# Two graph convolutions of a network block on one core: the sums of all destination blocks stay in seven PSUM banks, ScalarE makes the one-hots, SyncE counts landed tiles

## The chip, the cores and the metric

The program runs on one core of one Trainium2 chip. The metric is the device time of the whole program in microseconds (us), median of several runs; lower is better. The profile is one execution of the same program, recorded by the hardware profiler.

## The reference, cut to what matters

The whole reference is a two-layer network on 6250 nodes of 256 values with 100000 edges. Each layer adds a graph operator and a linear-attention mixer to the nodes, then a mixture-of-experts network. The part that changes is the graph operator of the second layer (two convolutions of width 64) and the mixer that is computed beside it:

```python
def gcn_conv(x, W, b, src, dst, n_nodes):
    h = x @ W
    deg = jax.ops.segment_sum(ones, dst, num_segments=n_nodes) + 1.0
    dinv = jax.lax.rsqrt(deg)
    norm = dinv[src] * dinv[dst]
    msg = h[src] * norm[:, None]
    agg = jax.ops.segment_sum(msg, dst, num_segments=n_nodes)
    agg = agg + h * (dinv * dinv)[:, None]
    return agg + b
h1 = jax.nn.relu(gcn_conv(embedding, W1, b1, src, dst, n))
h2 = jax.nn.relu(gcn_conv(h1, W2, b2, src, dst, n))
...
k = _ln(k, kln_g, kln_b); v = _ln(v, vln_g, vln_b)
kv = jnp.einsum('bhnd,bhne->bhde', k, v) / HW
...
h = jax.nn.gelu(ret @ w1 + b1, approximate=False)
return h @ w2 + b2 + bias
```

Everything is float32. The kernel sums rows of 64 values in both convolutions: the table of the first holds `dinv * (x @ W1)`, that of the second `dinv * relu(...)`, and `W2` is applied afterwards in another stage.

## The kernel before

The program is a row of stages with a barrier of all engines between them. `convolve` (L1806) is called twice, with `which` 0 and 1. Nodes are in `NB` = 49 blocks of 128. Edges are sorted by destination and cut into `NT` = 782 tiles of 128 edges, in `TG` = 98 groups of 8. A tile that spans two blocks is used once for each, so there are `NS` = 832 steps in `NG` = 104 groups of `GS` = 8; tables made earlier (`tabs`) say for each step which block it adds to (`blocks_of`, L371), in which slot of a ring of 96 tiles its rows are (`slots_of`, L376), and for each group of steps how many tile groups must have landed (`tiles_needed`, L381). On an engine such a table is read by a load into registers.

What each engine does in a convolution:

- **GpSimd (POOL)** gathers: one indirect DMA for each of the 782 tiles, 128 rows of 64 values from the table `t_d` in HBM into a ring slot (L1857). Before group g of tiles it waits until group g-2 has landed and adds one to `tiles_in`; from the fifth group on it also waits until step group g-5 has been summed (`summed`), so that a slot is free.
- **VectorE (DVE)** makes the one-hots of a step group in one instruction (L1924, `oh`, two buffers), and adds each of the 8 products of a step group from PSUM to the block's sum in SBUF (L1935, `m.agg`), each behind the one before. It also does the mixer's work of a block (`variance`, `scale`, `add_bias`, or `normalise`, `finish`). At the start it copies the table into `m.agg` (L1906). At the end of the first convolution `refresh` makes the next table, which SyncE stores.
- **TensorE (PE)** multiplies a one-hot (weights) by the gathered rows of a step (L2080, `total`), 8 steps to a PSUM bank, two banks in turn. It waits for the one-hots, for the adds of two groups before (`added`) and for `tiles_in`. Between an even and an odd step group stand the mixer's products of one block.
- **ScalarE (ACT)** does only the mixer's activations (square and root, or gelu).
- **SyncE (SP)** loads the weights, and the transposed nodes of one block at a time (L1894, `xt`).

The order on an engine is that of the code: `pipeline` writes a software-pipelined loop with one pass for two step groups and one mixer block; a pair is (lag, work).

Of the kernel before, what the change touches and what calls it, by code (L numbers as in the profile page):

```python
# [15 lines left out]
P = 128  # L16
# [11 lines left out]
GS = 8  # L28
# [1777 lines left out]
def convolve(nc, m, a, which):  # L1806
# [4 lines left out]
    with ExitStack() as ctx:  # L1811
# [5 lines left out]
        oh = sb("oh", [P, 2, GS, P])  # L1817
        xt = sb("xt", [P, D])
        bank = [ctx.enter_context(nc.psum_tensor(f"v{which}_bank{i}", [P, 512], F32)) for i in range(8)]
        s = {n: m.sem(f"v{which}_" + n) for n in "in0 in1 tiles_in oh_ready summed added started xt_in weights".split()}  # L1820
        landed = [s["in0"], s["in1"]]
        iota = bank[3 + which][:, 0:P]
        table = m.t_d.rearrange("b p n -> (b p) n")
        if which == 0:
# [5 lines left out]
            b1row = sb("b1row", [P, MH])  # L1830
            s.update({n: m.sem("v0_" + n) for n in ("chain centred kv_made kvb_ready squared summed16 var_ready std_ready rstd_ready "
                                                    "kn_ready kv_used scaled biased table stored sums_out").split()})
            mixed = s["kv_made"]
        else:
# [7 lines left out]
            t_ps, m2_ps = (bank[i][:, :].rearrange("p (c d) -> p c d", c=KC) for i in (5, 6))  # L1842
            s.update({n: m.sem("v1_" + n) for n in ("ht_made ht_ready out_made xn_ready xb_ready mixed res_ready "
                                                    "fold_in chain kvt t_made t_back m2_made folded").split()})
            mixed = s["ht_made"]

        with nc.Block() as block:
            @block.gpsimd
            def _(pool):
                for g in range(TG):  # L1850
                    if g >= 2:
                        pool.wait_ge(landed[g % 2], 16 * GS * (g // 2))
                        pool.sem_inc(s["tiles_in"], 1)
                    if g + NB // GS + 2 > RING // GS:
                        pool.wait_ge(s["summed"], g + NB // GS + 2 - RING // GS)
                    for t in range(g * GS, min((g + 1) * GS, NT)):
                        nc.gpsimd.indirect_dma_start(rows[:, t % RING, :], None, table,  # L1857
                                                     bass.IndirectOffsetOnAxis(ap=m.srct[:, t:t + 1], axis=0)).then_inc(landed[g % 2], 16)
                for g in (TG - 2, TG - 1):
                    pool.wait_ge(landed[g % 2], 16 * (GS * (g // 2) + min(GS, NT - g * GS)))  # L1860
                    pool.sem_inc(s["tiles_in"], 1)

            @block.sync
            def _(sp):
# [26 lines left out]
                def load(k, u, r):  # L1891
                    if at_least(k, 1):
                        sp.wait_ge(mixed, k)
                    sp.dma_start(xt[:, :], block_rows(m.xnt_d, k)).then_inc(s["xt_in"], 16)  # L1894
                pipeline(sp, NB, 1, (0, load))
                if which == 0:
                    for c in range(NB // 7):
                        sp.wait_ge(s["table"], c + 1)
                        sp.dma_start(m.t_d[7 * c:7 * c + 7].rearrange("b p n -> p b n"), m.table[:, 7 * c:7 * c + 7, :]).then_inc(s["stored"], 16)
                    sp.wait_ge(s["stored"], 16 * (NB // 7))  # L1900

            @block.vector
            def _(dve):
                V = nc.vector
                V.tensor_copy(iota, m.iota[:, :]).then_inc(s["started"], 1)
                V.tensor_copy(m.agg[:, :, :], m.table[:, :, :]).then_inc(s["started"], 1)  # L1906
                dve.wait_ge(s["started"], 2)
# [12 lines left out]

                def one_hot(g, u):
                    if at_least(g, 2):
                        dve.wait_ge(s["summed"], g - 1)
                    V.tensor_tensor(oh[:, u, :, :], iota.unsqueeze(1).to_broadcast([P, GS, P]),  # L1924
                                    m.dl[:, bass.ds(g * GS, GS)].unsqueeze(2).to_broadcast([P, GS, P]),
                                    ALU.is_equal).then_inc(s["oh_ready"], 1)

                def add(g, u):
                    dve.wait_ge(s["summed"], g + 1)
                    blocks = blocks_of(nc, m, mybir.EngineType.DVE, g * GS, GS)  # L1930
                    for k in range(GS):
                        t = g * GS + k
                        if at_least(t, 1):
                            dve.wait_ge(s["added"], t)
                        V.tensor_tensor(of_block(m.agg, blocks[k]), of_block(m.agg, blocks[k]), bank[u][:, k * MH:(k + 1) * MH],  # L1935
                                        ALU.add).then_inc(s["added"], 1)
# [24 lines left out]
                def add_bias(k, u, r):  # L1961
# [3 lines left out]
                    V.tensor_tensor(kvb[:, :, :, :].rearrange("p t h d -> p (t h d)"), bank[2][:, :],  # L1965
# [10 lines left out]
                def finish(k, u, r):  # L1976
                    dve.wait_ge(s["xb_ready"], k + 1)
                    dve.wait_ge(s["out_made"], k + 1)
                    V.tensor_tensor(xb[:, :], xb[:, :], bank[3][:, 0:D], ALU.add).then_inc(s["mixed"], 1)
# [5 lines left out]
                def refresh():  # L1985

                    dve.wait_ge(s["added"], NS)
                    part = lambda t, c: t[:, 7 * c:7 * c + 7, :]
                    dinv = lambda c: m.dinv[:, 7 * c:7 * c + 7].unsqueeze(2).to_broadcast([P, 7, MH])
                    n = NB // 7  # L1990
                    for c in range(n + 2):
                        if c < n:
                            V.tensor_tensor(part(m.agg, c), part(m.agg, c), dinv(c), ALU.mult).then_inc(s["scaled"], 1)
                        if 0 <= c - 1 < n:
                            dve.wait_ge(s["scaled"], c)
                            V.tensor_tensor(part(m.agg, c - 1), part(m.agg, c - 1), b1row[:, :].unsqueeze(1).to_broadcast([P, 7, MH]),
# [6 lines left out]
                def fold():  # L2003
# [9 lines left out]
                    for q in range(KC):  # L2013
# [12 lines left out]
                    V.tensor_tensor(m.c2[:, :], b1[:, :], bank[7][:, 0:KC], ALU.add).then_inc(s["folded"], 1)  # L2026

                conv = ((0, lambda k, u, r: one_hot(2 * k, 0)), (1, lambda k, u, r: add(2 * k + 1, 1)),
                        (0, lambda k, u, r: one_hot(2 * k + 1, 1)), (0, lambda k, u, r: add(2 * k, 0)))
                if which == 0:  # L2030
                    pipeline(dve, NR, 1, conv[0], conv[1], (1, variance, NB), conv[2], conv[3], (1, scale, NB), (0, add_bias, NB))
                    refresh()
                else:
                    fold()
                    dve.wait_ge(s["weights"], 32)
                    pipeline(dve, NR, 1, conv[0], conv[1], (1, normalise, NB), conv[2], conv[3], (1, finish, NB))

            @block.scalar
            def _(act):
                def root(k, u, r):  # L2040
# [11 lines left out]
                def gelu(k, u, r):  # L2052
# [3 lines left out]
                    for q in range(KC):  # L2056
                        last = nc.scalar.activation(ht[:, q, :], bank[2][:, q * P:(q + 1) * P], ACT.Gelu, bias=m.c2[:, q:q + 1])  # L2057
                    last.then_inc(s["ht_ready"], 1)
                if which == 0:
                    pipeline(act, NB, 1, (1, root), (0, square))  # L2060
                    act.wait_ge(s["kv_used"], NB)
                    for q in range(KC):
                        nc.scalar.copy(m.gram[:, q, 0:P + 1], bank[4 + q][:, 0:P + 1]).then_inc(s["sums_out"], 1)
                        nc.scalar.copy(m.gram[:, q, P + 1:2 * P + 1], bank[6 + q][:, 0:P]).then_inc(s["sums_out"], 1)
                    act.wait_ge(s["sums_out"], 2 * KC)
                else:
                    act.wait_ge(s["folded"], 2)
                    pipeline(act, NB, 1, (0, gelu))

            @block.tensor  # L2070
            def _(pe):
                def total(g, u):
                    pe.wait_ge(s["oh_ready"], g + 1)
                    if at_least(g, 2):
                        pe.wait_ge(s["added"], GS * (g - 1))
                    tiles = tiles_needed(nc, m, mybir.EngineType.PE, g)
                    at = slots_of(nc, m, mybir.EngineType.PE, g * GS, GS)
                    pe.wait_ge(s["tiles_in"], tiles)
                    for k in range(GS):
                        last = nc.tensor.matmul(bank[u][:, k * MH:(k + 1) * MH], oh[:, u, k, :], of_block(rows, at[k]),  # L2080
                                                start=True, stop=True)
                    last.then_inc(s["summed"], 1)

                def project(k, u, r):
# [3 lines left out]
                    for q in range(KC):  # L2088
                        last = nc.tensor.matmul(bank[2][:, :], xt[:, q * P:(q + 1) * P],
# [3 lines left out]
                def sum_kv(k, u, r):  # L2093
                    rows_ = LAST if isinstance(k, int) and k == NB - 1 else P
                    first, final = isinstance(k, int) and k == 0, isinstance(k, int) and k == NB - 1
                    pe.wait_ge(s["kn_ready"], 2 * k + 2)
                    for q in range(KC):

                        nc.tensor.matmul(bank[4 + q][:, 0:P + 1], vn[0:rows_, q * P:(q + 1) * P], kn[0:rows_, q, :],
                                         start=first, stop=final)  # L2100
                        last = nc.tensor.matmul(bank[6 + q][:, 0:P], m.ones[0:rows_, :], kn[0:rows_, q, 0:P],
                                                start=first, stop=final)
                    last.then_inc(s["kv_used"], 1)

                def up(k, u, r):
                    pe.wait_ge(s["xt_in"], 16 * (k + 1))
                    if at_least(k, 1):
                        pe.wait_ge(s["ht_ready"], k)
                    for j in range(KC):
                        for q in range(KC):  # L2110
                            last = nc.tensor.matmul(bank[2][:, j * P:(j + 1) * P], m.m2[:, q, j * P:(j + 1) * P],
# [3 lines left out]
                def down(k, u, r):  # L2115
                    pe.wait_ge(s["ht_ready"], k + 1)
                    if at_least(k, 1):
                        pe.wait_ge(s["mixed"], k)
                    for q in range(KC):
                        last = nc.tensor.matmul(bank[3][:, 0:D], ht[:, q, :], w2[:, q, :], start=(q == 0), stop=(q == KC - 1))  # L2120
# [3 lines left out]
                if which == 0:  # L2124
                    pe.wait_ge(s["centred"], 1)
# [610 lines left out]
```

## Time and profile before

| | us |
|---|---|
| timed runs, median of 3 (lowest, highest) | 5357.61 (5348.63, 5358.73) |
| span of the profiled execution | 5935.3 |
| in it, first convolution (2876 to 4088.3) | 1212.3 |
| in it, second convolution (4088.3 to 5279.6) | 1191.3 |
| engine busy over the span: PE, DVE, ACT, POOL | 3546.3, 2982.8, 1018.9, 3055.9 |

No time of the profiled execution other than its span is given; the span is 577.7 us above the median of the timed runs. Busy times are of instructions, and an engine that is not busy may wait for a semaphore or for its own queue. The granted clock is a share of the full TensorE clock of 2.4 GHz.

### The profile page before, as it was taken

The numbers are of one execution on the slowest core, as the hardware profiler recorded it, in microseconds if no ns is written. First come the engines' busy times: TensorE is split into PE (matmuls) and PEld (weight loads), VectorE is DVE, ScalarE is ACT, GpSimd is POOL, SyncE is SP. The second block draws the span as 40 slices with busy tenths as digits, with TensorE's granted clock in tenths as the row PEclk, the third lists the DMA queues.
The fourth block names the chain that finished last, engine by engine and source line by source line (L and its number), as shares of the span: only waits on it lengthen the run. The fifth ranks groups of instructions, "written<-read, shape, count | busy, mean of one in ns | idle before, by whom it ended". The sixth has DMA issues, their size and how long they took to land. (4 is left out here: it accounts for less than half of the span.)

```text
span 5935.3 us, 66919 instructions
## 1 busy us (share of the span) xinstructions
PE 3546.3 (60%) x13782; PEld 2710.2 (46%) x13783; DVE 2982.8 (50%) x6982; ACT 1018.9 (17%) x2146; POOL 3055.9 (51%) x2888
## 2 busy tenths in 40 slices
PE   4744455454389865998444544454445454466998
PEld 3633233232267654776433433333434444455666
DVE  5466566666899964445433333334333333354443
ACT  0111121121179801221000000000000000013121
POOL 1266677676368624221466666663666666612111
PEclk9877767776599976998566566655555555566999
DMA  4487666666578762223311111111111111123221
GB/s 108 136 217 211 202 207 203 204 206 195 158 227 271 224 188 88 63 63 97 106 28 28 29 28 28 29 29 32 28 29 28 28 29 28 29 62 98 70 87 37
DMA packets 432122, 617.01 MB, mean 104 GB/s; under 512 B 100329, under 2 KB 309161, under 8 KB 431721
## 3 DMA queue, kind: packets, MB, share of 16 engines
q1 hardware_dynamic: 304733, 389.03, 21.1%
q0 software_dynamic: 107440, 200.97, 14.1%
q10 hardware_dynamic: 19852, 25.94, 1.6%
q8 instruction: 33, 0.54, 0.0%
q14 instruction: 64, 0.52, 0.0%
HBM read 419.67 MB, written 209.64 MB: 106 GB/s over the span
## 5 line engine op out<-in xcount | busy, mean ns | idle before, releaser
L1857 POOL DMA_INDIRECT big<-t_d,src_tiles x1564 | 1483.7, 949 | 957.2 <-issue 450.8
L2080 PE MATMUL v_bank<-big,v_oh 128*128 x3328 | 716.2, 390 | 1216.6 <-issue 830.3
L2080 PEld LDWEIGHTS v_bank<-big,v_oh 128*128 128x128 f32 x3328 | 674.7, 300 | 1302.8 <-issue 1302.2
L653 POOL DMA_INDIRECT big<-xl_d,src_steps x832 | 859.8, 1033 | 378.1 <-issue 356.0
L1935 DVE TENSOR_TENSOR big<-big,v_bank 128x64 f32 x1664 | 366.5, 220 | 1285.3 <-DMA xj_d<-big 973.2
L759 PE MATMUL se_z_ps<-big,se_oht 128*128 x1664 | 608.7, 517 | 628.5 <-issue 385.9
L759 PEld LDWEIGHTS se_z_ps<-big,se_oht 128*128 128x128 f32 x1664 | 386.8, 250 | 850.4 <-issue 780.7
L692 DVE TENSOR_TENSOR se_z<-se_z_ps,big 128x528 f32<-128x528 f32 x416 | 291.4, 700 | 461.1 <-DMA es_ts<-src_p 256.8
L1122 PE MATMUL ae_bank<-ae_v,ae_oh 128*128 128x266 f32 x1664 | 402.3, 397 | 49.8 <-DVE big L1106 36.7
L1081 POOL TENSOR_TENSOR ae_v<-ae_v,ex 128x1792 f32<-128x1792 f32 x104 | 334.1, 3215 | 178.1 <-DMA ae_v<-xj_d 178.0
L1122 PEld LDWEIGHTS ae_bank<-ae_v,ae_oh 128*128 128x128 f32 x1664 | 310.4, 191 | 141.5 <-DVE big L1106 53.0
L1106 DVE TENSOR_TENSOR big<-big,ae_bank 128x266 f32 x832 | 303.8, 425 | 13.2 <-PE ae_bank L1122 7.5
L1924 DVE TENSOR_TENSOR v_oh<-v_bank,dl_steps 128x1024 f32<-128x1024 f32 x208 | 253.7, 1220 | 92.5 <-issue 92.0
L729 ACT ACTIVATE se_oht<-se_dlb,se_place 128x1024 f32<-128x1024 bf16 x104 | 119.4, 1148 | 986.6 <-DMA es_ts<-src_p 498.3
L700 DVE SCALAR_TENSOR_TENSOR se_w<-se_z,se_attb 128x512 f32<-128x512 f32 x416 | 284.8, 685 | 0.1
L1599 POOL DMA_INDIRECT y_d<-e_y,e_idx x106 | 104.1, 982 | 348.1 <-DVE e_idx L1562 328.6
L705 DVE TENSOR_REDUCE ex<-se_w 128x512 f32 (+1 forms) x416 | 281.6, 677 | 0.0
L2526 POOL DMA_INDIRECT out<-e_y,e_idx x64 | 63.0, 984 | 422.3 <-DVE e_y L2569 407.6
L1069 ACT ACTIVATE ae_oh<-iota,dl_steps 128x128 f32<-128x128 f32 x832 | 254.5, 388 | 60.0 <-PE ae_bank L1122 51.7
L2622 PE MATMUL e_bank<-big,e_ht 128*128 128x256 f32 x1024 | 225.3, 381 | 0.7 <-issue 0.7
L2611 PE MATMUL e_bank<-e_xt,big 128*128 128x465 f32 (+1 forms) x512 | 214.4, 577 | 1.6 <-DVE e_xt L2545 1.6
L2057 ACT ACTIVATE v_ht<-v_bank,c 128x128 f32<-128x128 f32 x98 | 30.6, 363 | 1064.8 <-remote 780.8
(468 smaller groups left out, 5316.9 us busy)
## 6 DMA issues: line engine op xcount, KB each, us to landing
xj_d<-big SPq DMA_DIRECT2D x208, 528.0 KB
ae_v<-xj_d SPq DMA_DIRECT2D x208, 528.0 KB
se_dlb<-dlr_d SPq DMA_DIRECT2D x104, 256.0 KB
big<-t_d,src_tiles POOLq DMA_INDIRECT x1564
buf_d<-ne_blank SPq DMA_DIRECT2D x4, 4112.0 KB
e_xs<-buf_d SPq DMA_DIRECT2D x106, 129.0 KB, 2.1
big<-xl_d,src_steps POOLq DMA_INDIRECT x832
cp_y<-y_d SPq DMA_DIRECT2D x14, 896.0 KB, 7.4
```

The source lines that it names most:

```text
L653: nc.gpsimd.indirect_dma_start(half_of(u)[:, k, :], None, table, bass.IndirectOffsetOnAxis(ap=m.src[:, t:t + 1], axis=0)).then_inc(landed[ ...
L692: nc.vector.tensor_tensor(z[:, u, k:k + 2, :], z_ps[v % 4][:, :, 0:LW], xj[:, u, k:k + 2, :], ALU.add).then_inc(s["z_ready"], 1)
L700: nc.vector.scalar_tensor_tensor(w[:, v % 2, :, :], z[:, u, k:k + 2, 0:D], 0.0, wide, ALU.max, ALU.mult).then_inc(s["weighed"], 1)
L705: nc.vector.tensor_reduce(m.ex[:, bass.ds(q * 2 * H, 2 * H)], w[:, v % 2, :, :].rearrange("p k (h c) -> p (k h) c", h=H), AX.X, ALU.add)\
L759: last = nc.tensor.matmul(z_ps[v % 4][:, i, 0:LW], oht[:, u, k + i, :], of_block(m.xr, blocks[2 * (v % 2) + i]), start=True, stop=True)
L1069: nc.scalar.activation(oh[:, w % 2, k, :], m.iota[:, :], ACT.Abs, bias=m.dl[:, bass.ds(g * GS + k, 1)], scale=-1.0).then_inc(s["oh_apart"], 1)
L1081: nc.gpsimd.tensor_tensor(x, x, ex, ALU.mult).then_inc(s["high_ready"], 1)
L1106: V.tensor_tensor(to, to, bank[k][:, 0:AW], ALU.add).then_inc(s["added"], 1)
L1122: nc.tensor.matmul(bank[k][:, 0:AW], oh[:, w % 2, k, :], v[:, w, k, :], start=True, stop=True)\
L1857: nc.gpsimd.indirect_dma_start(rows[:, t % RING, :], None, table, bass.IndirectOffsetOnAxis(ap=m.srct[:, t:t + 1], axis=0)).then_inc(lande ...
L1935: V.tensor_tensor(of_block(m.agg, blocks[k]), of_block(m.agg, blocks[k]), bank[u][:, k * MH:(k + 1) * MH], ALU.add).then_inc(s["added"], 1)
L2080: last = nc.tensor.matmul(bank[u][:, k * MH:(k + 1) * MH], oh[:, u, k, :], of_block(rows, at[k]), start=True, stop=True)
```

## The change

Four things change in `convolve`, in both convolutions:

- The sums of all 49 blocks stay in seven PSUM banks (`sums`, 8 blocks of 64 values to a bank, the last holding one block and small sums of the mixer). TensorE fills them from the table at the start (`seed`), and every product then accumulates into its block's place, whose address comes from a register. VectorE's 832 adds, the wait on `added` and the copy at the start go.
- The mixer has one bank (`side`) left. Its column sums are one-column products, spread to rows after the loop.
- The one-hots are made by ScalarE, in nine instructions for a group: eight times |iota - dl| and once relu(1 - x). The mixer's activations stand behind them in the same queue.
- SyncE, not GpSimd, waits for landed tiles and counts `tiles_in`, in the same queue as the loads of `xt`.

The core of the diff (the mixer's sums and the ends of the stages shortened):

```diff
-                        pool.sem_inc(s["tiles_in"], 1)
...
-                def load(k, u, r):
-                    if at_least(k, 1):
-                        sp.wait_ge(mixed, k)
+                def load(k):
                     sp.dma_start(xt[:, :], block_rows(m.xnt_d, k)).then_inc(s["xt_in"], 16)
-                pipeline(sp, NB, 1, (0, load))
+
+                def tiles_landed(k, u, r):
+                    for i in range(2):
+                        sp.wait_ge(landed[i], 16 * GS * (k + 1))
+                        sp.sem_inc(s["tiles_in"], 1)
+                    sp.wait_ge(mixed, k + 1)
+                    load(k + 1)
+                load(0)
+                pipeline(sp, NB - 1, 1, (0, tiles_landed))
...
-                V.tensor_copy(iota, m.iota[:, :]).then_inc(s["started"], 1)
-                V.tensor_copy(m.agg[:, :, :], m.table[:, :, :]).then_inc(s["started"], 1)
...
-                    pipeline(dve, NR, 1, conv[0], conv[1], (1, variance, NB), conv[2], conv[3], (1, scale, NB), (0, add_bias, NB))
+                    pipeline(dve, NB, 1, (1, variance), (1, scale), (0, add_bias))
                     refresh()
...
-                    pipeline(dve, NR, 1, conv[0], conv[1], (1, normalise, NB), conv[2], conv[3], (1, finish, NB))
+                    pipeline(dve, NB, 1, (0, normalise), (0, finish))
+                    dve.wait_ge(s["summed"], NG)
+                    for c in range(NK // 2):
+                        V.tensor_copy(m.agg[:, PB * c:PB * c + PB, :], agg[:, PB * c:PB * c + PB, :]).then_inc(s["agg_out"], 1)
...
+                def one_hot(g, u):
+                    if at_least(g, 2):
+                        act.wait_ge(s["summed"], g - 1)
+                    for k in range(GS):
+                        nc.scalar.activation(oh[:, u, k, :], m.iota[:, :], ACT.Abs, bias=m.dl[:, bass.ds(g * GS + k, 1)],
+                                             scale=-1.0).then_inc(s["oh_apart"], 1)
+                    act.wait_ge(s["oh_apart"], GS * (g + 1))
+                    nc.scalar.activation(oh[:, u, :, :], oh[:, u, :, :], ACT.Relu, bias=m.ones[:, 0:1], scale=-1.0)\
+                        .then_inc(s["oh_ready"], 1)
...
-                    pipeline(act, NB, 1, (1, root), (0, square))
+                    pipeline(act, NR, 1, even, odd, (2, root, NB), (1, square, NB))
...
-                    pipeline(act, NB, 1, (0, gelu))
+                    pipeline(act, NR, 1, even, odd, (1, gelu, NB))
...
+                def seed():
+                    for c in range(NK):
+                        lo, hi = PB * c, min(PB * c + PB, NB)
+                        nc.tensor.matmul(agg[:, lo:hi, :].rearrange("p b n -> p (b n)"), m.ident[:, :],
+                                         m.table[:, lo:hi, :].rearrange("p b n -> p (b n)"), start=True, stop=True)
+
                 def total(g, u):
                     pe.wait_ge(s["oh_ready"], g + 1)
-                    if at_least(g, 2):
-                        pe.wait_ge(s["added"], GS * (g - 1))
                     tiles = tiles_needed(nc, m, mybir.EngineType.PE, g)
                     at = slots_of(nc, m, mybir.EngineType.PE, g * GS, GS)
+                    to = blocks_of(nc, m, mybir.EngineType.PE, g * GS, GS)
                     pe.wait_ge(s["tiles_in"], tiles)
                     for k in range(GS):
-                        last = nc.tensor.matmul(bank[u][:, k * MH:(k + 1) * MH], oh[:, u, k, :], of_block(rows, at[k]),
-                                                start=True, stop=True)
+                        last = nc.tensor.matmul(of_block(agg, to[k]), oh[:, u, k, :], of_block(rows, at[k]),
+                                                start=False, stop=True, skip_group_check=True)
...
-                    pipeline(pe, NR, 1, even, (1, down, NB), (0, up, NB), odd)
+                    seed()
+                    pipeline(pe, NR, 1, even, (0, up, NB), odd, (0, down, NB))
```

TensorE's queue in the loop of the second convolution, before, from the last product of the even step group to the first of the odd one (`v_w`, `v_ht`, `v_xt`, `m` are the mixer's operands, `tabs` the tables of steps; ISA rows are register operations):

```order
L2080 MATMUL v_bank<-big,v_oh 128x64
L2118 REGISTER_ALU
L2120 MATMUL v_bank<-v_w,v_ht 128x256 x2
L2106 ISA
L2111 MATMUL v_bank<-v_xt,m 128x128 x4
L2073 REGISTER_ALU
L383 ISA
L383 TENSOR_LOAD tabs
L383 ISA x2
L378 ISA
L378 TENSOR_LOAD tabs
L2080 ISA
```

The same place in the changed kernel (`v_side` is the mixer's bank):

```order
L2131 ISA
L2136 MATMUL v_side<-v_xt,m 128x128 x4
L2100 REGISTER_ALU
L383 ISA
L383 TENSOR_LOAD tabs
L383 ISA x2
L378 ISA
L378 TENSOR_LOAD tabs
L373 ISA
L373 TENSOR_LOAD tabs
L2106 ISA
L2106 REGISTER_ALU
```

The second product of the mixer (L2120 before, L2143 now) has moved from between the two step groups to the end of the pass; each step group has one more table load (L373), and each step one more register operation ahead of its product.

ScalarE's loop of the second convolution, before, whole (`v_ht` is the gelu's output):

```order
L112 UNCONDITIONAL_BRANCH
L112 ISA
L2057 ACTIVATE v_ht<-v_bank,c 128x128 x2
L112 REGISTER_ALU
L112 COMPARE_AND_BRANCH
```

and the end of a pass of the same loop in the changed kernel (`ex` holds the one-hots now):

```order
L2042 ISA
L2042 ACTIVATE ex<-iota,dl_steps 128x128
L2044 ISA
L2045 ACTIVATE ex<-ex,ones 128x1024
L2063 REGISTER_ALU
L2065 ACTIVATE v_ht<-v_side,c 128x128 x2
L112 REGISTER_ALU
L112 COMPARE_AND_BRANCH
```

Ahead of these rows stand the rest of the sixteen L2042 activations and the other L2045 of the pass: the gelu of a block is now behind the one-hots of both step groups of the next pass.

## Rows read from the trace of the kernel before

**Rows 1.** Busy time by engine in six stretches; then PEclk, DMA share, GB/s.
```profile
core 0: us, PE busy (x) PEld busy (x) DVE busy (x) ACT busy (x) POOL busy (x), PEclk, DMA share, GB/s
0.00:239.30 239.30, 158.22 (x746) 133.69 (x747) 119.04 (x318) 19.76 (x51) 24.54 (x33) 0.96 0.39 102
239.30:1490.00 1250.70, 608.65 (x1664) 386.76 (x1664) 782.47 (x1356) 240.06 (x209) 861.64 (x838) 0.72 0.70 205
1490.00:2876.00 1386.00, 1087.00 (x4650) 824.36 (x4650) 967.85 (x2234) 535.83 (x1384) 573.31 (x331) 0.85 0.51 157
2876.00:4088.30 1212.30, 560.49 (x2252) 456.62 (x2252) 438.47 (x1266) 42.20 (x102) 743.32 (x782) 0.60 0.15 29
4088.30:5279.60 1191.30, 563.88 (x2272) 502.25 (x2272) 389.12 (x1148) 31.88 (x99) 740.34 (x782) 0.55 0.14 28
5279.60:5935.30 655.70, 568.02 (x2198) 406.48 (x2198) 285.81 (x661) 149.19 (x301) 112.76 (x123) 0.87 0.25 79
```

**Rows 2.** The gathers of the first convolution, then of the second.
```profile
L1857 POOL DMA_INDIRECT big<-t_d,src_tiles x782: 938/944/2229, 2878.4 to 4011.6; - x196
  DMA xj_d<-big: 163.5, 59
...
L1857 POOL DMA_INDIRECT big<-t_d,src_tiles x782: 938/944/2203, 4089.0 to 5220.0; - x196
  DMA xj_d<-big: 160.6, 44
```

**Rows 3.** Timeline of the second convolution, one held-up pass, then its release.
```profile
4623.46 1.30 PE L2111 MATMUL v_bank<-v_xt,m 128*128 128x128 f32 x8
4624.70 0.94 POOL L1857 DMA_INDIRECT big<-t_d,src_tiles  x1 [0.30 <-issue]
...
4632.31 0.27 PE L2080 MATMUL v_bank<-big,v_oh 128*128 x1 [2.54 <-issue]
...
4634.03 0.63 ACT L2057 ACTIVATE v_ht<-v_bank,c 128x128 f32<-128x128 f32 x2 [22.52 <-remote]
4634.11 0.94 POOL L1857 DMA_INDIRECT big<-t_d,src_tiles  x1 [3.47 <-DMA xj_d<-big]
```

**Rows 4.** Timeline of PE after the first convolution's last gather.
```profile
4028.44 3.67 PE L2080 MATMUL v_bank<-big,v_oh 128*128 x16 [2.39 <-DVE big L1935]
...
4033.73 3.44 PE L2089 MATMUL v_bank<-v_wkv,v_xt 128*128 128x512 f32 x4
...
4040.49 3.67 PE L2080 MATMUL v_bank<-big,v_oh 128*128 x16 [1.59 <-issue]
```

**Rows 5.** The gathers of the stage from 239.3, grouped by line.
```profile
L653 POOL DMA_INDIRECT big<-xl_d,src_steps x832 | 859.8, 1033 | 378.1 <-issue 356.0 <-DVE se_z L692 20.6 <-DMA xj_d<-big 1.5
```

**Rows 6.** Timeline of the two ends: last adds, what follows.
```profile
4070.78 2.76 DVE L1935 TENSOR_TENSOR big<-big,v_bank 128x64 f32 x8 [2.46 <-PE v_bank L2080]
4073.58 1.16 DVE L1993 TENSOR_TENSOR big<-big,dinv 128x448 f32<-128x448 f32 x2
...
5275.75 2.76 DVE L1935 TENSOR_TENSOR big<-big,v_bank 128x64 f32 x8 [2.42 <-PE v_bank L2080]
```

**Rows 7.** PE's table loads between 4022 and 4072, ns.
```profile
L378 PEldq TENSOR_LOAD <-tabs x9: 585/589/597, 4022.0 to 4065.6; - x9
...
L383 PEldq TENSOR_LOAD <-tabs x8: 302/304/310, 4026.9 to 4064.8; - x8
```

**Rows 8.** Timeline of ACT in an earlier stage that makes one-hots so.
```profile
1886.56 2.45 ACT L1069 ACTIVATE ae_oh<-iota,dl_steps 128x128 f32<-128x128 f32 x8
1889.04 1.15 ACT L1072 ACTIVATE ae_oh<-ae_oh,ones 128x1024 f32<-128x1024 f32 x1
```

**Rows 9.** Groups of the first convolution, then of the second, by line.
```profile
L2080 PE MATMUL v_bank<-big,v_oh 128*128 x1664 | 337.2, 377 | 625.8 <-issue 365.5 <-DVE big L1935 259.8
...
L2080 PE MATMUL v_bank<-big,v_oh 128*128 x1664 | 379.1, 403 | 590.8 <-issue 464.8 <-DVE big L1935 116.1 <-DVE v_oh L1924 8.0
...
L1906 DVE COPY big<-big 128x3136 f32<-128x3136 f32 x1 | 1.8, 1781 | 0.0
```

More of the change, by code:

```diff
@@ L1830, in convolve @@
             b1row = sb("b1row", [P, MH])
+            ksum, kwide = sb("ksum", [P, KC]), sb("kwide", [P, KC, P])
+            last = sums[:, NK - 1, :, :].rearrange("p b n -> p (b n)")
+            kv_ps = [last[:, MH + 136 * q:MH + 136 * q + P + 1] for q in range(KC)]
+            ksum_ps = last[:, MH + 136 * KC:MH + 136 * KC + KC]
             s.update({n: m.sem("v0_" + n) for n in ("chain centred kv_made kvb_ready squared summed16 var_ready std_ready rstd_ready "
-                                                    "kn_ready kv_used scaled biased table stored sums_out").split()})
+                                                    "kn_ready kv_used scaled biased table stored sums_out wide spread").split()})
             mixed = s["kv_made"]
@@ L2056, in gelu @@
                     for q in range(KC):
[L2057 removed]
+                        last = nc.scalar.activation(ht[:, q, :], h_ps[:, q * P:(q + 1) * P], ACT.Gelu, bias=m.c2[:, q:q + 1])
                     last.then_inc(s["ht_ready"], 1)
+                even, odd = (0, lambda k, u, r: one_hot(2 * k, 0)), (0, lambda k, u, r: one_hot(2 * k + 1, 1))
                 if which == 0:
[L2060 removed]
+                    pipeline(act, NR, 1, even, odd, (2, root, NB), (1, square, NB))
@@ new lines, in _ @@
+                    act.wait_ge(s["sums_out"], 1)
+                    for q in range(KC):
+                        nc.scalar.activation(kwide[:, q, :], m.iota[:, :], ACT.Identity, bias=ksum[:, q:q + 1], scale=0.0).then_inc(s["wide"], 1)
+                    act.wait_ge(s["spread"], 1)
+                    for q in range(KC):
+                        nc.scalar.copy(m.gram[:, q, P + 1:2 * P + 1], side[:, q * P:(q + 1) * P]).then_inc(s["sums_out"], 1)
+                    act.wait_ge(s["sums_out"], 2 * KC + 1)
@@ L2066, in _ @@
                 else:
                     act.wait_ge(s["folded"], 2)
-                    pipeline(act, NB, 1, (0, gelu))
+                    pipeline(act, NR, 1, even, odd, (1, gelu, NB))
+                    act.wait_ge(s["summed"], NG)
+                    for c in range(NK // 2, NK):
+                        lo, hi = PB * c, min(PB * c + PB, NB)
+                        nc.scalar.copy(m.agg[:, lo:hi, :], agg[:, lo:hi, :]).then_inc(s["agg_out"], 1)
+                    act.wait_ge(s["agg_out"], NK)
@@ L2124, in _ @@
                 if which == 0:
+                    seed()
                     pe.wait_ge(s["centred"], 1)
                     pipeline(pe, NR, 1, even, (2, sum_kv, NB), (0, project, NB), odd)
+                    pe.wait_ge(s["wide"], KC)
+                    for q in range(KC):
+                        last = nc.tensor.matmul(side[:, q * P:(q + 1) * P], kwide[:, q, :], m.ident[:, :], start=True, stop=True)
+                    last.then_inc(s["spread"], 1)
                 else:
```

102 lines of the change are left out of this document (45 added, 57 removed).

## The prediction

> **What bounds the kernel now.** I read the stretches first [rows 1]. The two convolutions take 1212.3 and 1191.3 us, 40% of the span, and in both POOL is the busiest engine, with 743 and 740 us, while PE has 560, DVE 438 and 389, ACT 42 and 32. Then the gathers by themselves [rows 2]: 782 in a convolution, 0.944 us each, and 0.30 us between one and the next [rows 3]. A gather thus costs POOL 1.25 us, and a convolution cannot be shorter than 743.3 + 781 x 0.30 = 977.6 us of gathers. The first gather starts at 2878.4 and the last at 4011.6, which is 1134 us with its own length; the rest is 163.5 us in 59 waits. They are put down to a DMA, but what ended them is PE's count `summed`, for the ring of slots: the timeline shows it [rows 3]. PE had the mixer's product (L2111, from 4623.46, 1.30 long) issued long before, yet the gelu that waits for it starts at 4634.03, and POOL goes on at 4634.11, after 3.47 us. All that waited for PE is released in the same tenth of a microsecond, some 9 us late. So in this execution PE's signals come late by whole microseconds, POOL stops every pass or second pass for 3 or 4 us, and PE is behind when the last gather is done.
>
> After the last gather the delays are gone: one pass of the loop with two step groups and a block of the mixer takes 4040.49 - 4028.44 = 12.05 us [rows 4], where POOL needs 977.6 / 52 = 18.8 us for a pass. PE and DVE alone would be well ahead of POOL.
>
> **Does the timed run have these delays?** This decides the sum, since the profiled span is 5935.3 us and the timed median 5357.6: 577.7 us are only in the profiled execution. The work outside gather loops is 239.3 + 1386 + 655.7 = 2281 us, and there PE is busy 158, 1087 and 568 us, DVE 968 of the 1386 [rows 1]: I see no place for 578 us of slack. In the gather loops there is one. Waits of POOL in the convolutions: 163.5 + 160.6 [rows 2] = 324. PE's arrears at their ends: from 4012.6 to the end of the last add at 4073.5 are 61 us, from 5221 to 5278.5 are 57.5 [rows 2, 6]. With PE up to date the end needs two step groups of 3.67 + 1.59 (the second number is its idle time before a group, register work) [rows 4], 0.8 us and 2.76 of adds [rows 6], and about 2 us for landing (my estimate, nothing here shows it), in all 16. So 45 + 42 = 87 are arrears. The earlier gather stage has 859.8 + 378.1 us [rows 5] against 859.8 + 831 x 0.30 = 1109, which is 129 more. Together 324 + 87 + 129 = 540 of 577.7. I take it that the recording delays PE's signals, and that the timed kernel is bound by POOL's 1.25 us for a gather in both convolutions, about 1000 us each. This is inferred from one sum, not seen.
>
> **The change part by part**, against that timed kernel:
>
> - *Gathers* stay as they are: 782 by 1.25 us, from the barrier on, behind the same waits. POOL's increment of `tiles_in` goes, an operation of its queue that costs it nothing between gathers (0.30 us, with or without one). 0 us.
> - *Copies at DVE's start* go. The first gather of each convolution takes 2.229 and 2.203 us instead of 0.944 [rows 2], beside the copy of 1.8 us [rows 9]. If the copy holds it, that gives 2 x 1.27 = -2.5 us. All gathers together are 743.3 + 740.3 - 1564 x 0.944 = 7.2 us above the median [rows 1, 2], so no more than -7.2 can come from here. The Trainium skill, "SBUF — State Buffer", section "Who interferes with whom", says that DVE and GpSimd share a port that a float32 copy locks, so that gathers issued by GpSimd wait. By that rule the gain would be between these two numbers, and the trace agrees for the first gather.
> - *DVE's adds*, 2.76 us for a group [rows 6], lie beside POOL's 18.8 us for two groups; only the last ones are on the path. The last eight take 4073.58 - 4070.78 = 2.8 us to `refresh` [rows 6], and ahead of them DVE loads the blocks' numbers, about 0.8 (an estimate from PE's 0.59 for such a load [rows 7]); together 3.6, and as much at the end of the second. -3.6 and -3.6. Against it: one more table load of 0.59 [rows 7] before the last step group, +0.6 twice; in the second convolution the sums are copied out of PSUM, three banks on DVE and four on ACT at once. A pass over 448 columns takes 0.58 (two in 1.16 [rows 6]), so 512 take 0.66, three or four of them 2.0 to 2.6: +2.3. `refresh` handles the same number of columns from PSUM: 0.
> - *Seed*: 7 products, six of 512 columns. Two of 512 took 3.44 us at the lower clock [rows 4], so about 11. In the first convolution the first eight gathers take 10 us anyway; in the second they start after the mixer's folding, some 22 us behind, while POOL has four step groups (38 us) of room in the ring. 0 us.
> - *One-hots on ACT*: from 1886.56 to 1890.19, 3.63 us a group [rows 8]. Two groups and the mixer's activations are some 8.2 us of ACT in 18.8. Hidden, if the ring through the engines closes in time; here is what is queued. In the second convolution the gelu of block k stands behind the one-hots of step groups 2k+2 and 2k+3, and the latter wait for PE's group 2k+1 (two buffers). PE's `down` waits for the gelu, and all step groups behind it. One pass is: odd step group 3.67 [rows 4], one-hots 3.63 [rows 8], gelu 0.63 [rows 3], `down` beside the register work of the next group, 1.59 and a further 0.59 = 2.2 [rows 4, 7], even group 3.67, `up` (1.30) beside 2.2, signals 0.4: 16.4 us. That is under 18.8. With the register work beside nothing it is 16.4 + 1.3 for `up` and about 2 for `down` = 19.7. At the full clock the two groups take half as long, 12.7; PEclk is 0.55 to 0.60 here, near the lower level of 1.2 GHz [rows 1], so I take 16.4. In the first convolution the ring is odd group 3.67, one-hots 3.63, root and scaling about 1.5, the mixer's sums 2 (both my estimates: three short operations of DVE, and eight products of at most 129 columns, as many as in L2111's 1.30 [rows 3]), projection 3.44 [rows 4], signals 0.4: 14.7. Both hidden: 0 us.
> - *SyncE's counting*: it loads the next `xt` only when the two tile groups of its pass have landed, and counts no further ones before PE's mixer product of the pass. PE needs neither earlier: its step groups 2k and 2k+1 need at most tile groups up to 2k+1. 0 us.
>
> Sum: -2.5 - 7.2 + 1.2 + 2.3 = -6.2, so 5357.6 - 6.2 = 5351. The difference is 0.12%, less than the 0.2% (10.7 us) that a measurement of this kernel can about tell from none; the three runs themselves lie 10 us apart.
>
> **The rivals.**
>
> 1. *No difference that can be told* (my forecast): 5351, with 5346 to 5362 as its own range. Chance 0.55.
> 2. *The pass of the second convolution gets longer than POOL's.* Mechanism: gelu behind one-hots behind the odd step group. For it speak the new order of both queues and that only 2.4 us are left between 16.4 and 18.8; against it that the register work ran beside the mixer's products before. It decides from 18.8 us on, and costs 49 us for each microsecond beyond. At 19.7 that is 0.9 x 49 = 44, less 6: 5396. Chance 0.20, with further 0.03 for a ring in the first.
> 3. *The delays are real in timed runs too.* Then PE waited for adds 259.8 + 116.1 us [rows 9], which go. In the first convolution this exceeds POOL's waits and arrears, 163.5 + 45 = 208; in the second 116 are left. With the 6: 5357.6 - 208 - 116 - 6 = 5028. Against it speaks the sum of 540 above. Chance 0.11.
> 4. *DVE's relief gives POOL all that it lost*: -7.2 instead of -2.5, and the copies at the end cost 1 less: 5351 - 4.7 - 1 = 5345, just beyond the bound. Chance 0.11.
>
> **How the numbers follow.** The likeliest is 5351. Faster by over 0.2%: rivals 3 and 4, 0.22. Slower: rival 2, 0.23. The same: 0.55. The range goes from 5330 (rival 4 with a few us more, since part of the gaps of 0.30 might close) to 5400 (the upper end of the ring, 19.7); it leaves out rival 3 and a tenth for worse rings.
>
> **What the changed kernel's profile would show.** Gathers still at 0.944 and 0.30, the first no longer 2.2. DVE busy in the convolutions down from 438 and 389 by more than half, ACT up by 104 x 3.6 = 374 each. From PE's last product to `refresh` under 1 us. Its span, again, far above its timed runs, with POOL still waiting for PE: if the recording is what delays PE, more instructions on PE's queue may even lengthen it. In the second convolution PE idle 4 to 5 us before each `down`. I am wrong if POOL waits in timed runs: if the timed kernel falls by 50 us or more, the delays were real; if it rises by 20 or more, the ring of rival 2 has closed late.

## The result and the profile after

| | median us (lowest, highest) | ratio to before [95%] |
|---|---|---|
| before, same chip | 5357.51 (5348.63, 5358.73) | |
| changed kernel | 5384.94 (5379.73, 5388.05) | 1.0056 [1.0042, 1.007] |

It is 27 us slower by the medians, and 30 by the ratio (23 to 38). The prediction said 5351, and that is wrong: the difference is clear of zero and of the other sign.

The span of the profiled execution is 5382.5 us now, so it agrees with the timed runs and holds none of the 578 us of before's profile. Before can therefore not be compared with it through [rows 1 to 9]. I recorded the unchanged kernel again (label e4_before_again, below), and its span is 5357.6. These are the four stretches from its first gather on: first convolution, what lies between, second convolution, its end (columns as in [rows 1]).

```profile
2691.00:3680.00 989.00, 542.23 (x2233) 443.47 (x2233) 421.81 (x1225) 42.21 (x102) 739.53 (x782) 0.61 0.16 33
3680.00:3706.40 26.40, 4.66 (x21) 4.28 (x20) 17.11 (x44) 0.00 (x0) 0.00 (x0) 0.50 0.28 62
3706.40:4695.50 989.10, 523.98 (x2252) 484.73 (x2252) 384.08 (x1126) 31.96 (x99) 740.31 (x782) 0.57 0.16 33
4695.50:4708.00 12.50, 4.91 (x22) 4.54 (x21) 5.55 (x22) 0.00 (x0) 0.22 (x4) 0.50 0.02 3
```

The same four of the changed kernel:

```profile
2684.00:3674.00 990.00, 566.95 (x2177) 443.55 (x2178) 129.96 (x303) 392.76 (x998) 740.84 (x782) 0.57 0.16 33
3674.00:3714.00 40.00, 21.57 (x95) 20.43 (x94) 13.03 (x26) 15.71 (x44) 0.16 (x1) 0.50 0.19 42
3714.00:4702.00 988.00, 557.92 (x2193) 486.20 (x2193) 87.11 (x210) 385.45 (x999) 738.93 (x782) 0.51 0.16 34
4702.00:4732.00 30.00, 21.38 (x95) 20.40 (x94) 2.71 (x8) 16.05 (x40) 1.10 (x9) 0.50 0.01 2
```

From the first gather to the last, both convolutions take what they took, 987 to 989 us, and POOL waits for TensorE 0.3 us in all before and 1.5 us after: POOL sets the pace in both kernels. What grows is the stretch *after* the last gather. POOL sits idle 40.67 us between the convolutions instead of 26.81, and the next stage starts 28.83 us after the second one's last gather instead of 12.28. That is 13.9 + 16.5 = 30.4 us. TensorE shows why: 95 products there instead of 21 and 22. This is its timeline behind the changed kernel's last gather (end at 3674.16), and what releases DVE's `refresh` and POOL:

```profile
3660.40 3.78 PE L2115 MATMUL v_side<-v_wkv,v_xt 128*128 128x512 f32 x4 [6.81 <-DMA v_xt<-xnt_d]
...
3674.68 3.65 PE L2106 MATMUL v_sums<-big,ex 128*128 x16 [0.32 <-issue]
3679.70 3.65 PE L2106 MATMUL v_sums<-big,ex 128*128 x16 [1.38 <-issue]
...
3685.51 3.65 PE L2106 MATMUL v_sums<-big,ex 128*128 x16 [0.40 <-issue]
3689.43 3.65 PE L2106 MATMUL v_sums<-big,ex 128*128 x16 [0.28 <-issue]
3695.01 3.64 PE L2106 MATMUL v_sums<-big,ex 128*128 x16 [1.94 <-issue]
...
3698.69 1.29 DVE L1990 TENSOR_TENSOR big<-v_sums,dinv 128x512 f32<-128x512 f32 x2 [15.52 <-PE v_sums L2106]
...
3714.83 0.94 POOL L1865 DMA_INDIRECT big<-t_d,src_tiles  x1 [40.67 <-POOLq L134]
```

Five whole step groups are still to do, and the last ends 24.5 us after the last gather. The same place in the kernel before, recorded again (last gather's end at 3679.67): the end of one group and one more, which ends 7.8 us after.

```profile
3683.80 3.67 PE L2080 MATMUL v_bank<-big,v_oh 128*128 x16 [2.81 <-DVE big L1935]
...
3688.26 2.76 DVE L1935 TENSOR_TENSOR big<-big,v_bank 128x64 f32 x8 [3.33 <-PE v_bank L2080]
3691.06 1.16 DVE L1993 TENSOR_TENSOR big<-big,dinv 128x448 f32<-128x448 f32 x2
...
3706.48 2.21 POOL L1857 DMA_INDIRECT big<-t_d,src_tiles  x1 [26.81 <-POOLq L134]
```

What holds TensorE up shows in the changed kernel's waits of 2690 to 3660 (in total, times, longest):

```profile
ACT ex L2042 <- PE v_sums L2106: 490.2, 76, 12.7
...
PE v_sums L2106 <- SPq L1902: 248.2, 60, 9.8
...
PE v_side L2115 <- DMA v_xt<-xnt_d: 128.8, 19, 9.0
...
POOL big L1865 <- PE v_sums L2106: 1.5, 5, 0.3
```

L1902 is SyncE's count of landed tiles; TensorE has to wait for this count in either kernel. The wait for the load of `xt` is the new one: in the kernel before, recorded again, nothing waits for it (L2089 and L2111 have no idle time before them). Where it stands in time says why it matters. Of its 19 waits in the first convolution none lies before 3100 and only two before 3300; the waits for SyncE's count fall in turn, from 19 between 2690 and 2900 to none after 3500. In the second convolution the 19 waits (54.5 us) all come after 4300. So TensorE first waits for tiles that it needs, and later for a load that stands behind tiles that it does not need yet. SyncE issues the load for the last block at 3658.32, TensorE's projection waits 6.81 us for it, and seven of the 104 step groups stand behind. The last projection of the kernel before, recorded again, came 50 us before the last gather's end and not 14:

```profile
3629.28 2.37 PE L2089 MATMUL v_bank<-v_wkv,v_xt 128*128 128x512 f32 x4
```

POOL hardly waits for TensorE: the sign that rival 2 needed is not there.

### The profile page after: what moved, and what is told of

It reads as the page before. It is cut to its first block and busy times, and to the rows that moved or that the text cites. A ratio compares the mean times of both kernels' runs of the same rounds, so it can differ in the third digit from the quotient of the medians.

```text
span 5382.5 us, 67089 instructions
## 1 busy us (share of the span) xinstructions
PE 3628.2 (67%) x13814; PEld 2767.8 (51%) x13815; DVE 2394.1 (44%) x5109; ACT 1756.3 (33%) x4025; POOL 3025.4 (56%) x2888
## 5 line engine op out<-in xcount | busy, mean ns | idle before, releaser
L1865 POOL DMA_INDIRECT big<-t_d,src_tiles x1564 | 1480.3, 946 | 635.4 <-issue 495.1
L2106 PE MATMUL v_sums<-big,ex 128*128 x3328 | 700.5, 398 | 431.8 <-SPq L1902 338.8
L653 POOL DMA_INDIRECT big<-xl_d,src_steps x832 | 831.5, 999 | 253.9 <-issue 242.6
L2106 PEld LDWEIGHTS v_sums<-big,ex 128*128 128x128 f32 x3328 | 676.4, 307 | 543.4 <-issue 543.3
L759 PE MATMUL se_z_ps<-big,se_oht 128*128 x1664 | 658.4, 564 | 425.2 <-issue 335.5
L2042 ACT ACTIVATE ex<-iota,dl_steps 128x128 f32<-128x128 f32 x1664 | 507.9, 387 | 1129.4 <-PE v_sums L2106 1085.4
L759 PEld LDWEIGHTS se_z_ps<-big,se_oht 128*128 128x128 f32 x1664 | 440.4, 279 | 643.1 <-issue 548.5
L1974 DVE TENSOR_TENSOR v_xb<-v_xb,v_side 128x256 f32<-128x256 f32 x49 | 20.6, 421 | 868.0 <-PE v_side L2143 868.0
L1946 DVE RECIPROCAL v_rstd<-v_std 128x16 f32<-128x16 f32 x49 | 12.4, 253 | 800.9 <-ACT v_std L2052 800.9
L2115 PE MATMUL v_side<-v_wkv,v_xt 128*128 128x512 f32 x196 | 177.8, 1061 | 135.6 <-DMA v_xt<-xnt_d 135.6
L2143 PE MATMUL v_side<-v_w,v_ht 128*128 128x256 f32 x196 | 101.7, 674 | 212.7 <-ACT v_ht L2065 212.7
```

What stands on the lines that cost most here:

```text
L653: nc.gpsimd.indirect_dma_start(half_of(u)[:, k, :], None, table, bass.IndirectOffsetOnAxis(ap=m.src[:, t:t + 1], axis=0)).then_inc(landed[ ...
L759: last = nc.tensor.matmul(z_ps[v % 4][:, i, 0:LW], oht[:, u, k + i, :], of_block(m.xr, blocks[2 * (v % 2) + i]), start=True, stop=True)
L2042: nc.scalar.activation(oh[:, u, k, :], m.iota[:, :], ACT.Abs, bias=m.dl[:, bass.ds(g * GS + k, 1)], scale=-1.0).then_inc(s["oh_apart"], 1)
L2106: last = nc.tensor.matmul(of_block(agg, to[k]), oh[:, u, k, :], of_block(rows, at[k]), start=False, stop=True, skip_group_check=True)
```

## The experiments

There are two sets of runs, each with its own runs of the kernel before: 5357.37 us in the first (e1 to e4), 5361.79 in the second (e5, e7 to e9). Ratios are to before in the same set, with a 95% interval. A *tail* is the time from the end of a convolution's last gather to the end of its last step group on TensorE; in the changed kernel the two tails are 24.5 and 25.9 us, in the kernel before 7.8 and 7.6.

**e4_before_again: the kernel before, unchanged.**

> The kernel before, unchanged, profiled once more. Theory R (the recording itself holds PE's signals back in this kernel): the span is again near 5935 and POOL again waits over 100 us in each convolution. Theory X (that one recorded execution was held up, the recording does not do it as such): the span is within 5 us of the timed 5357.5, POOL waits for PE under 10 us in each convolution, and the last add of a convolution ends 14 to 18 us after the last gather.

5359.3 us, span 5357.6. POOL does not wait for `summed` any more. Its gathers in the first convolution, then those of the stage of [rows 5]:

```profile
L1857 POOL DMA_INDIRECT big<-t_d,src_tiles x782 | 739.5, 946 | 347.0 <-issue 231.6 <-POOLq L134 98.3 <-DMA big<-t_d,src_tiles 17.1
...
L653 POOL DMA_INDIRECT big<-xl_d,src_steps x832 | 835.7, 1004 | 255.8 <-issue 241.7 <-DMA xj_d<-big 12.9 <-DVE se_z L692 1.2
```

The 163.5 us of [rows 2] are gone: the 17.1 us put down to a DMA here are gaps of 0.30 us, as long as any other between two gathers. In the stage of [rows 5] the idle time falls from 378.1 to 255.8. With a span that agrees with the timed runs, the timed kernel has none of the delays, as theory X said; only its tail was expected longer, 14 to 18 us to the last add where 11.4 were measured. Theory R falls too, that recording causes the delays: this recording and all the others, nine in number, lie within 12 us of their timed medians. Only that one execution was held up; why is open.

**e1_pool_counts: SyncE's part undone in the changed kernel.**

```diff
-                    for i in range(2):
-                        sp.wait_ge(landed[i], 16 * GS * (k + 1))
-                        sp.sem_inc(s["tiles_in"], 1)
...
                         pool.wait_ge(landed[g % 2], 16 * GS * (g // 2))
+                        pool.sem_inc(s["tiles_in"], 1)
```

> The changed kernel with GpSimd waiting for landed tiles and counting them again, and SyncE only loading xt. Theory A (SyncE's queue ties the load of xt for pass k+1 to the landing of tile groups 2k and 2k+1, so PE, which needs by then up to six tile groups fewer, ends each convolution with some five step groups still to do instead of two): the ends shorten by 8 to 12 us each, 5384.9 falls by 16 to 26 us to 5359 to 5369, and PE no longer waits for xt. If the shorter last link (no adds) also pays, 5350 to 5358. Theory B (ScalarE's one-hots in the ring are what makes PE late): 5380 to 5390, no change.

5353.70 us, ratio 0.9993 [0.9983, 1.0002]. The last two groups of its first convolution (last gather's end at 3686.43); the tail is 7.4 us:

```profile
3684.63 3.65 PE L2101 MATMUL v_sums<-big,ex 128*128 x16 [0.26 <-issue]
3690.23 3.64 PE L2101 MATMUL v_sums<-big,ex 128*128 x16 [1.96 <-issue]
```

The whole loss is gone, and nothing waits for `xt` any more. Theory A holds, but it had the size too small: 8 to 12 us were expected from each end, and the tails fell by 17 and 18. The other three changes together are worth -3.7 us, not to be told from nothing.

**e2_sync_counts_only: SyncE's part alone, in the kernel before** (the same lines, other direction).

> The kernel before with one part of the change alone: SyncE waits for landed tiles and counts them, in the queue of the xt loads. Theory A: slower than before by 15 to 25 us, 5372 to 5382, with PE waiting for xt late in each convolution. Theory B: 5357, no change.

5387.17 us, 1.0054 [1.004, 1.0067]: the whole loss, without banks and without ScalarE's one-hots. It is 30 us, where 15 to 25 were expected, with TensorE waiting for `xt` 39 times, 302 us in all, and with tails of 23.2 and 22.3 us. TensorE behind the last gather of the first convolution (end at 3682.63):

```profile
3686.93 3.67 PE L2085 MATMUL v_bank<-big,v_oh 128*128 x16 [1.12 <-issue]
...
3692.30 3.67 PE L2085 MATMUL v_bank<-big,v_oh 128*128 x16
3696.73 3.67 PE L2085 MATMUL v_bank<-big,v_oh 128*128 x16 [0.75 <-issue]
3702.20 3.67 PE L2085 MATMUL v_bank<-big,v_oh 128*128 x16 [1.80 <-issue]
```

**e5_scalar_loads: SyncE still counts, ScalarE issues the loads.** Is it the counting, or the load behind it?

```diff
-                    sp.wait_ge(mixed, k + 1)
-                    load(k + 1)
...
+                    nc.scalar.dma_start(xt[:, :], block_rows(m.xnt_d, k)).then_inc(s["xt_in"], 16)
```

> The changed kernel with one move: SyncE still counts landed tiles, but the loads of xt are issued by ScalarE, in its own queue at the front of each pass, so that no load stands behind a landing any more. Theory A (the loss is the coupling of the two jobs in one queue, xt of block k+1 behind the landing of tile groups 2k and 2k+1): about 5354, like the version in which POOL counts; TensorE ends one to two step groups after the last gather, 7 to 9 us, instead of 5 to 6 groups and 25 us. Rival (SyncE's counting is itself late, wherever the loads are): about 5385, as the changed kernel. A third outcome, 5360 to 5375, if a load behind ScalarE's one-hots is late for TensorE.

5354.84 us, 0.9985 [0.9976, 0.9994], tails 7.4 and 7.4 us, as theory A said. Counting on SyncE costs nothing; only the two jobs in one queue do. This is the fastest variant against before, by 0.15%, which is less than the 0.2% of the prediction.

**e3_vector_one_hots: the changed kernel with one-hots on VectorE.** The iota comes from SBUF, since the bank that held it is taken.

```diff
+                    V.tensor_tensor(oh[:, u, :, :], m.iota[:, :].unsqueeze(1).to_broadcast([P, GS, P]),
+                                    m.dl[:, bass.ds(g * GS, GS)].unsqueeze(2).to_broadcast([P, GS, P]), ALU.is_equal)
```

> The changed kernel with the one-hots made by VectorE again (from iota in SBUF, in the order even, mixer, odd; ScalarE only does the mixer's activations). Theory A: 5378 to 5388, since SyncE's coupling stays; a few us less than 5384.9 at most, because a step group at the end then takes 4 us instead of 4.7. Theory B: falls to 5351 to 5360. Against both: if the instruction from SBUF to SBUF holds GpSimd off, gathers beside it get longer than 0.944 us and the time rises by up to 208 x 1 us.

5451.16 us, 1.0172 [1.0159, 1.0186], 66 us over the changed kernel and outside both theories' ranges; the third sentence of the expectation names what happened. TensorE's tails are 19.5 and 17.4 us, shorter than the changed kernel's by 13.5 in all, so the loss is not there; the gathers themselves got longer, 1560.5 us for both convolutions against 1480.3. 80.2 - 13.5 = 66.7, the whole difference.

**e7_before_sbuf_iota: the kernel before, iota from SBUF.** This asks whether it is the operand.

```diff
-                    V.tensor_tensor(oh[:, u, :, :], iota.unsqueeze(1).to_broadcast([P, GS, P]),
+                    V.tensor_tensor(oh[:, u, :, :], m.iota[:, :].unsqueeze(1).to_broadcast([P, GS, P]),
```

> The kernel before with one operand changed: VectorE's one-hots compare with the iota in SBUF instead of its copy in PSUM, so that both inputs come from SBUF. Theory P (an operation of VectorE with both inputs in SBUF holds GpSimd off, which is what lengthened the gathers in the changed kernel with one-hots on VectorE): the gathers' own busy time rises from 740 to about 775 to 785 us in each convolution and the time by 65 to 85, to 5425 to 5440. Rival (the 66 us there came from the order of VectorE's queue, one-hots behind the mixer's work, or from the copy in PSUM that was missing at the start): gathers stay at 740 and the time at about 5357.

5437.5 us, 1.0137 [1.0121, 1.0152], 76 more, as theory P said. Its gathers and one-hots, both convolutions together:

```profile
L1857 POOL DMA_INDIRECT big<-t_d,src_tiles x1564 | 1566.6, 1002 | 620.6 <-issue 466.9 <-POOLq L134 125.4 <-DMA big<-t_d,src_tiles 28.4
...
L1924 DVE TENSOR_TENSOR v_oh<-iota,dl_steps 128x1024 f32<-128x1024 f32 x208 | 253.6, 1220 | 2.2
```

and those of the kernel before, recorded again:

```profile
L1857 POOL DMA_INDIRECT big<-t_d,src_tiles x1564 | 1479.8, 946 | 622.5 <-issue 462.3 <-POOLq L134 125.1 <-DMA big<-t_d,src_tiles 34.8
...
L1924 DVE TENSOR_TENSOR v_oh<-v_bank,dl_steps 128x1024 f32<-128x1024 f32 x208 | 253.6, 1220 | 2.1
```

VectorE takes exactly as long, POOL 86.8 us longer: 0.42 us for each one-hot whose two inputs both come from SBUF. So in this layout, where no PSUM bank is left for the iota, ScalarE's one-hots earn their place: not against VectorE's time, but against the longer gathers. The Trainium skill, "SBUF — State Buffer", "Who interferes with whom", says that a VectorE instruction with two SBUF inputs contends with a GpSimd instruction that reads SBUF. If a gather is one that reads SBUF, where its row numbers lie, both runs had to lose by that rule, and the trace agrees. The same section of the Trainium skill infers that such a tensor_tensor does not hold up the making of a DMA's descriptors; the 0.42 us here speak against that for gathers, and the measurement decides.

**e8_two_more and e9_four_more: how far is rival 2's ring from the bound?** On e1, with more work for ScalarE behind each step group's one-hots (2, then 4):

```diff
+                    for j in range(2):
+                        nc.scalar.activation(spare[:, :, :], m.iota[:, :].unsqueeze(1).to_broadcast([P, GS, P]), ACT.Relu)
```

> The changed kernel with POOL counting (5354 us), and two further activations of 128x1024 on ScalarE behind each step group's one-hots, 1.15 us each and about 0.1 for a wait, which write to a spare buffer: 5.0 us more in a pass. It asks how far the ring of gelu, one-hots and step groups is from the bound. With the ring as I reckoned it (16.4 us a pass in the second convolution, 14.7 in the first, against 19.0 of POOL): 21.4 and 19.7, so 2.4 x 49 = 118 and 0.7 x 49 = 34 more, about 5505. With a ring of 14 or less in both: no change, 5354. In between, the rise of each convolution over 989 us divided by 49 gives ring minus 19.0.

> The same with four further activations for each step group, 10 us more in a pass. With my rings of 16.4 and 14.7: 26.4 and 24.7, so 7.4 x 49 + 5.7 x 49 = 640 more, about 5995. If nothing but ScalarE's own sum binds (7.3 of one-hots, 10 of extra work, 1 of the mixer = 18.3 in a pass): about 5354 to 5370. The difference to the version with two shows whether each further microsecond costs 49 us in a convolution, as it must once the ring is the bound.

e8: 5358.19 us, 0.9993 [0.9984, 1.0003], no change, where 5505 was expected. e9: 5555.95 us, 1.0356 [1.034, 1.0371], where 5995 was expected; its first convolution still takes 992.8 us from first to last gather, its second 1102.0, with TensorE 93 us behind at the end. The gelus alone, of three passes on end, first of e8, then of e9, show the closed ring, 18.57 and 22.9 us:

```profile
3826.70 0.61 ACT L2066 ACTIVATE v_ht<-v_side,c 128x128 f32<-128x128 f32 x2
...
3845.26 0.61 ACT L2066 ACTIVATE v_ht<-v_side,c 128x128 f32<-128x128 f32 x2
...
3863.83 0.61 ACT L2066 ACTIVATE v_ht<-v_side,c 128x128 f32<-128x128 f32 x2
```

```profile
3836.50 0.61 ACT L2066 ACTIVATE v_ht<-v_side,c 128x128 f32<-128x128 f32 x2
...
3859.42 0.61 ACT L2066 ACTIVATE v_ht<-v_side,c 128x128 f32<-128x128 f32 x2
...
3882.29 0.61 ACT L2066 ACTIVATE v_ht<-v_side,c 128x128 f32<-128x128 f32 x2
```

Each extra activation is some 1.05 us, so without the four or eight of a pass the ring is 14.4 or 14.5. Without extra work, in e1, the gelus of passes in which TensorE catches up come 14.6 to 14.9 or 16.1 us apart. The pass of 16.1 in e1, PE, then ACT:

```profile
4624.26 2.08 PE L2138 MATMUL v_side<-v_w,v_ht 128*128 128x256 f32 x4 [4.32 <-ACT v_ht L2060]
4627.27 3.65 PE L2101 MATMUL v_sums<-big,ex 128*128 x16 [0.94 <-issue]
4630.71 2.02 PE L2131 MATMUL v_side<-v_xt,m 128*128 128x128 f32 x8
4632.53 3.52 PE L2101 MATMUL v_sums<-big,ex 128*128 x16
```

```profile
4636.17 2.44 ACT L2037 ACTIVATE ex<-iota,dl_steps 128x128 f32<-128x128 f32 x8 [1.48 <-PE v_sums L2101]
4638.64 1.15 ACT L2040 ACTIVATE ex<-ex,ones 128x1024 f32<-128x1024 f32 x1
4639.70 0.61 ACT L2060 ACTIVATE v_ht<-v_side,c 128x128 f32<-128x128 f32 x2
```

It is the chain of the prediction link by link: `down`, even group, `up`, odd group, one-hots, gelu. In the pass before it the odd group took 2.20 us, at a granted clock of 0.87 instead of 0.50, and the pass 14.7. My expectations added the extra work to this chain and were wrong by 147 us for e8 and 439 for e9: with it ScalarE's two sets of one-hots stand one behind the other after the even group, and the odd group lies beside them, so the ring grows from 14.4 and not from 16.1 or 16.4. At 18.6 it stays under POOL's 19.0; in e9 it is 3.9 over, and 48 x 3.9 = 187 are nearly all of its 198 us over e8. Gathers and tail of the second convolution say the same: 1102.0 - 990.5 and 93.3 - 7.4 are 197. In the first convolution the 8.4 us more of e9 cost nothing (992.8 against 991.2 in e8), so adding them to the 14.7 reckoned for its ring was wrong too; that ring itself was not measured.

## Why the prediction was wrong, step by step

- **"SyncE's counting: ... PE needs neither earlier. 0 us."** This step failed, and it is the whole error of sign. It compares step groups 2k and 2k+1 with tile groups up to 2k+1 and finds them covered, but that is an upper limit. There are 104 step groups and 98 tile groups. With free counting, step group g needs about tile group 98/104 x g (an estimate that spreads the steps evenly), so at the end the 49th block's pass (step groups 96 and 97) could run with tile groups to about 91 landed. The load of the 49th `xt` stands behind the landing of tile groups 94 and 95 and ties the pass to that. It goes out at 3658.32, when the last 14 of 782 gathers have just begun, but seven of 104 step groups are still to do. From the projection at 3660.40 these take until 3698.65, 38.2 us; the last gather ends 13.8 us after it, so the tail is 24.5. It is paid at both ends. e2 shows that this part alone costs it all, e1 and e5 that all of it comes back without it. The prediction had no rival for this step, and its sign for a rise of 20 or more pointed to the ring of rival 2, which was not the cause.
- **Gathers bound both convolutions: right.** 977.6 was reckoned, 988 measured from first gather to last in e4, and 987 to 992 in every kernel whose gathers were left at 0.944 and that had TensorE in time. The 10.6 us between these two are six gaps of 1.9 to 2.3 us in each convolution, some 142 us apart, in both kernels and wherever the count is; nothing in the traces says what they are.
- **Delays only in the profiled execution: right in effect, wrong in its cause** (e4). Rival 3 falls: 5028 was never near. And "its span, again, far above its timed runs" was wrong. The prediction's "signals" come late is also too narrow: in the pass of [rows 3] TensorE's own products came one at a time, at 4626.71, 4629.51 and 4632.31.
- **Copies at the start, -2.5, bound -7.2: seen at the first gathers, not in the sum.** These take 1.00 and 0.94 us instead of 2.23 and 2.21 in e4, -2.5 together. But all 1564 take 1480.3 us against 1479.8, so the others were 3 us longer, and no net gain shows. So rival 4 falls too; of the 7.2 only 3.4 are there in e4 (1479.8 - 1564 x 0.944).
- **Ends, with PE up to date: mis-sized.** I took 16 us from the last gather to the last add. It is 11.4 in e4 (3691.02 - 3679.67), since little more than one group is late and not two. The term entered only the arrears, not the sum of -6.2.
- **Last adds, -3.6 each: right in the first convolution.** From the last product to `refresh` 3.59 us in e4 (3687.47 to 3691.06), 0.04 in the changed kernel. In the second convolution from the last product to GpSimd's first instruction of the next stage 4.7 before and 2.9 after, so -1.7 where -3.6 + 2.3 = -1.3 was said. With GpSimd counting (e1, e8) it is 4.7 and 4.8, and nothing is gained there; why these differ from e5's 2.9 is open.
- **One-hots hidden, ring of the second convolution 16.4: right in mechanism and size.** 16.1 measured, 14.6 to 14.9 where the clock rises, against 18.8 to 19.0. Some 4 us more of ScalarE's work are free in a pass (e8), 8.4 are not (e9). ScalarE's busy time rose by 351 and 353 us, where 374 were said. The seed took 8.3 and 5.6 us for the 11 reckoned, and nothing waited for it.
- **Sum: -6.2 was said of everything.** What holds without SyncE's part is -3.7 (e1, interval -9 to +1) and -7 (e5, -13 to -3).

The tails account for the loss: 24.5 - 7.8 = 16.7 in the first and 25.9 - 7.6 = 18.3 in the second, less 3.6 and 1.7 of the ends, are 29.7, of the 30.4 by which POOL's two idle times grew; the timed difference is 27.4 by the medians and 30 by the ratio.

## What to carry to other kernels

When a queue gets a second job, ask for the *last* passes, not the steady ones, how far the first job could have run ahead, and what is tied to it now: a wait that costs nothing while another engine is slower turns into arrears at the end. Two loops over different counts (49 blocks, 52 pairs of step groups, 49 of tile groups) drift apart, and the tie bites where the drift is largest: here all waits for `xt` came late in each convolution. And if a profile's span is far from the timed runs, record again before reasoning on its waits.

## What the runs showed of the hardware

- VectorE's one-hots with both inputs in SBUF lengthened GpSimd's gathers by 0.42 us for each one-hot instruction while their own 1.22 us stayed the same (e7): only the other engine's row shows it.
- One profiled execution was 578 us longer than the timed runs, with everything that waited for TensorE released late [rows 3]; nothing like it came back in nine further recordings.
- A queue of gathers, each 0.944 us long with 0.30 us to the next, has a gap of 1.9 to 2.3 us every 142 us or so, in e4, e1 and the changed kernel alike.
